# One transformer layer on one core: the last tiles' scaling on ScalarE, and four regroupings in the order of the work

## The reference

```
x = layernorm(x + attention(x))          # 2 x 1024 tokens, D = 512, 16 heads of 32, causal
x = layernorm(x + ffn(x))                # no gain or bias in either layer norm, eps 1e-5
attention: qkv = x @ w_qkv.T + b_qkv; softmax(q k.T / sqrt(32) + causal) v; @ w_out.T + b_out
ffn:  relu((x @ sign(up).T) * up_scale) @ sign(down).T * down_scale * output_scale   # 2048 hidden
```

## Time and profile before

| | |
|---|---|
| median of three runs | 750.09 us |
| the three runs | 747.69, 750.09, 751.0 us |
| the profiled execution | 748.02 us |
| its span, first to last instruction | 746.3 us |
| busy share of the span: PE, DVE, ACT, POOL | 96%, 56%, 43%, 50% |
| mean granted TensorE clock | 0.992 of full speed |

### The profile page before, as it was taken

The page is one execution under the profiler, slowest core; times in us unless marked ns, Lnnn a source line. Parts: engine busy times, 40 slices in busy tenths (PEclk is TensorE's granted clock), DMA queues, the critical chain, the costliest instruction groups (busy, mean ns, idle before and its releaser), DMA issues.

```text
span 746.3 us, 11995 instructions
## 1 busy us (share of the span) xinstructions
PE 714.2 (96%) x4136; PEld 513.9 (69%) x4136; DVE 419.1 (56%) x1024; ACT 323.9 (43%) x647; POOL 374.1 (50%) x515
## 2 busy tenths in 40 slices
PE   6899999999999999999999999999899999999994
PEld 4688766666666656666554677688688787878883
DVE  4176466475765838557388542445783368324514
ACT  5211355665556656556555687522322222222211
POOL 4561458395583946739405449551362245223334
PEclk9999999999999999999999999999999999999997
DMA  7975455625545356463767455313215101000101
GB/s 238 291 232 147 125 156 152 161 88 158 169 144 157 108 144 176 112 161 99 205 184 233 151 191 150 106 47 96 72 32 138 29 1 57 1 1 14 43 1 56
DMA packets 47796, 90.03 MB, mean 121 GB/s; under 512 B 5820, under 2 KB 14780, under 8 KB 47608
## 3 DMA queue, kind: packets, MB, share of 16 engines
q1 hardware_dynamic: 38712, 84.02, 37.9%
q10 hardware_dynamic: 9024, 5.24, 2.4%
HBM read 59.38 MB, written 29.61 MB: 119 GB/s over the span
## 4 chain that ended last, share of the span: by engine, by line
PE 86%; DVE 5%; DMA 3%; issue 3%; ACT 2%; POOL 1%; SPq 0%; ACTq 0%; DVEq 0%; POOLq 0%
PE ps_proj L1115 10%; PE ps_heads L1216 9%; PE ps_proj L1267 8%; PE ps_score L1292 7%; PE ps_unit L1267 7%; PE ps_unit L1151 6%; PE ps_unit L1183 5%; PE ps_unit L1238 5%; PE ps_sum L1210 5%; PE ps_score L1183 4%; PE ps_score L1151 4%; PE ps_sum L1292 2%; PE ps_heads L1292 2%; PE ps_unit L1292 2%; PE ps_score L1135 2%
## 5 line engine op out<-in xcount | busy, mean ns | idle before, releaser
L798 POOL TENSOR_TENSOR hid_low<-hid_raw,hid_high 128x512 fp32r<-128x512 f32 (+1 forms) x80 | 89.8, 1122 | 174.0 <-DVE hid_high L1049 165.9
L855 ACT ACTIVATE probs<-ps_unit 128x512 f32<-128x512 f32 (+3 forms) x214 | 102.2, 490 | 85.1 <-PE ps_unit L1183 80.9
L761 POOL TENSOR_SCALAR_AFFINE_SELECT probs<-probs 128x128 f32<-128x128 f32 x256 | 73.9, 304 | 79.8 <-ACT probs L855 76.0
L855 ACT ACTIVATE probs<-ps_score 128x512 f32<-128x512 f32 (+3 forms) x170 | 82.7, 496 | 64.7 <-PE ps_score L1183 61.8
L961 DVE CUSTOM_DVE_ANT_0 ps_unit<-ps_unit,causal 128x128 f32<-128x128 f32 (+3 forms) x162 | 80.5, 514 | 45.9 <-PE ps_unit L1151 45.2
L1049 DVE CAST hid_high<-hid_raw 128x512 fp32r<-128x512 f32 (+1 forms) x80 | 34.5, 432 | 127.7 <-ACT hid_raw L918 127.2
L1151 PE MATMUL ps_unit<-stack 96*128 96x512 f32 (+3 forms) x242 | 82.9, 354 | 4.4 <-DMA stack<-qk_parts 1.7
L1216 PE MATMUL ps_heads<-probs,v_rows 128*32 128x512 f32 (+3 forms) x768 | 79.8, 492 | 0.0
L1183 PE MATMUL ps_unit<-stack 98*128 98x512 f32 (+2 forms) x214 | 76.8, 362 | 0.6 <-ACT probs L855 0.5
L755 POOL TENSOR_TENSOR parts<-qk_full,parts 128x512 fp32r<-128x512 f32 x32 | 41.2, 1288 | 65.6 <-ACT parts L834 65.6
L774 POOL TENSOR_TENSOR added<-added,probs 128x512 f32<-128x512 f32 x56 | 71.8, 1291 | 0.0
(11 more groups left out here) (216 smaller groups left out, 1462.8 us busy)
## 6 DMA issues: line engine op xcount, KB each, us to landing
stack<-qk_parts SPq DMA_DIRECT2D x96, 256.0 KB, 4.7
qk_parts<-parts SPq DMA_DIRECT2D x32, 512.0 KB, 2.9
v_all<-h_even ACTq DMA_DIRECT2D x16, 256.0 KB, 3.4
v_rows<-v_all SPq DMA_DIRECT2D x8, 512.0 KB, 4.2
heads_t<-heads_sb SPq DMA_DIRECT2D x16, 256.0 KB, 2.6
x_tile<-x_rows SPq DMA_DIRECT2D x16, 256.0 KB, 4.8
raw<-up_w SPq DMA_DIRECT2D x8, 512.0 KB, 3.6
raw<-down_w SPq DMA_DIRECT2D x8, 512.0 KB, 3.9
```

Source lines behind the costliest of these rows:

```text
L761: nc.gpsimd.affine_select(out=tile, in_=tile, compare_op=ALU.is_ge, fill=0.0, base=0, pattern=[[1, P]], channel_multiplier=-1).then_inc(s_ ...
L798: nc.gpsimd.tensor_tensor(parts2[1][:, (HM * s + n) % 3, 0:tokens(s)], full[:, n % 2, 0:tokens(s)], parts2[0][:, (HM * s + n) % 3, 0:token ...
L855: nc.scalar.activation(probs[:, (NP * s + n) % RING, 0:width], bank(what, s, n)[:, off:off + width], ACT.Exp, scale=SCALE).then_inc(s_exp, 1)
```

## The change

Five things are changed.

1. For the last chunk, `out` no longer runs on DVE alone. DVE makes a small offset, `off2 = -mean * rstd` (one column), and ACT writes `z = z * rstd + off2` in place in `z_sb`; the store reads `z_sb`. The last four tiles no longer use `out_sb`. ACT's square root for these tiles is issued with `ln2` instead of with `out`. `mom2`, `std2` and `rstd2` have four columns instead of two, and the wait of the statistics for an older `out` is gone.
2. `ln2` and `out` of the first chunk's tiles 0 and 1 move from slots 12.0 to 13.9 of round 1 to slots 0.2, 0.7, 2.9 and 3.4 of the round behind it, which readers may count as the third (it carries the second chunk). The `scale` pieces of the third chunk start there 0.6 slots later.
3. The first chunk's `attn` of tile 0 starts 1.1 slots sooner, and its `y` 0.9 slots sooner. Its first four matmuls need only the high part of w_out, so the wait for the low part (`s_wol`) moves to the fifth.
4. The first chunk's `turn` pieces stand 0.5 to 0.7 slots later.
5. Round 0's `up` and `down` stand 0.5 and 0.4 slots later, 1.93 instead of 1.95 apart.

```diff
-            put((late + 44.6, late + 47.4, last + 2.4, last + 5)[i] + 0.22 * m, "attn", 0, 12 * i + m)
+            put((late + 43.5, late + 47.4, last + 2.4, last + 5)[i] + 0.22 * m, "attn", 0, 12 * i + m)
...
-        put((last + 13.2, last + 13.7, last + 14.8, last + 15.3)[i], "turn", 0, i)
+        put((last + 13.8, last + 14.4, last + 15.3, last + 15.9)[i], "turn", 0, i)
...
-                put(end + (1.05 if r else 10.8) + q, "ln2", i, q)
-                put(end + (1.95 if r else 11.7) + q, "out", i, q)
+                put(end + 1.05 + q if r else FIRST_UP + 16.2 + 2.7 * q, "ln2", i, q)
+                put(end + 1.95 + q if r else FIRST_UP + 16.7 + 2.7 * q, "out", i, q)
...
                     sp.wait_ge(s_o, TT * s + n + 1)
-                    sp.dma_start(out[s * HALF + n * P:s * HALF + (n + 1) * P, :], out_sb[:, n % 2, :]).then_inc(s_os[n % 2], 16)
+                    src = z_sb[:, n, :] if s == CH - 1 else out_sb[:, n % 2, :]
+                    sp.dma_start(out[s * HALF + n * P:s * HALF + (n + 1) * P, :], src).then_inc(s_os[n % 2], 16)
...
-                if what == "out":
+                if what == ("ln2" if s == CH - 1 else "out"):
                     act.wait_ge(s_mom2, TT * s + n + 1)
-                    nc.scalar.activation(std2[:, n % 2:n % 2 + 1], mom2[:, n % 2, 1:2], ACT.Sqrt, bias=eps[:, :]).then_inc(s_sq2, 1)
+                    nc.scalar.activation(std2[:, n:n + 1], mom2[:, n, 1:2], ACT.Sqrt, bias=eps[:, :]).then_inc(s_sq2, 1)
+                if what == "out" and s == CH - 1:
+
+                    act.wait_ge(s_off, n + 1)
+                    nc.scalar.activation(z_sb[:, n, :], z_sb[:, n, :], ACT.Identity, bias=off2[:, n:n + 1],
+                                         scale=rstd2[:, n:n + 1]).then_inc(s_o, 1)
...
                     dve.wait_ge(s_rs, rs)
+                    if s == CH - 1:
+
+                        nc.vector.tensor_scalar(off2[:, k], mom2[:, n, 0:1], rstd2[:, k], -1.0,
+                                                ALU.mult, ALU.mult).then_inc(s_off, 1)
+                        continue
                     wait(dve, s_os[n % 2], 16 * ((TT * s + n) // 2))
...
-                            pe.wait_ge(s_wol, 2)
...
+                    if s == 0 and n == DC:
+                        pe.wait_ge(s_wol, 2)
```

More of the change, by code:

```diff
@@ L229, in plan @@
         for m in range(12):
-            put((late + 44.6, late + 47.4, last + 2.4, last + 5)[i] + 0.22 * m, "attn", 0, 12 * i + m)
-        put((late + 47.3, last + 2.1, last + 5.1, last + 7.8)[i], "y", 0, i)
+            put((late + 43.5, late + 47.4, last + 2.4, last + 5)[i] + 0.22 * m, "attn", 0, 12 * i + m)
+        put((late + 46.4, last + 2.1, last + 5.1, last + 7.8)[i], "y", 0, i)
         put(last + 9.9 + 0.1 * i, "norm1", 0, i)
-        put((last + 13.2, last + 13.7, last + 14.8, last + 15.3)[i], "turn", 0, i)
+        put((last + 13.8, last + 14.4, last + 15.3, last + 15.9)[i], "turn", 0, i)
     put(last + 9.8, "std1", 0)
@@ L237, in plan @@
         for m in range(HM):
-            put(t + m if r else last + 15.6 + 1.95 * m, "up", r, m)
+            put(t + m if r else last + 16.1 + 1.93 * m, "up", r, m)
             if r < len(ROUNDS) - 1 or m < HM - 2:
-                put(t + m + 2.5 if r else last + 20.5 + 1.95 * m, "down", r, m)
+                put(t + m + 2.5 if r else last + 20.9 + 1.93 * m, "down", r, m)
         if r == len(ROUNDS) - 1:
@@ L243, in plan @@
                 put(t + 17, "finish", i, q)
-        end = t + 17.55 if r else FIRST_UP + 1.2
+        end = t + 17.55 if r else FIRST_UP + 1.6
         for q in tiles:
@@ L261, in plan @@
                 if i:
-                    put(t + (0.1 if i == 1 else -1.4) + 0.5 * q, "scale", i + 1, q)
+                    put(t + (0.7 if i == 1 else -1.4) + 0.5 * q, "scale", i + 1, q)
                 put(t + (2.2 + 0.7 * q if i else 0.3 * q - 0.8), "split", i + 1, q)
@@ L396, in build @@
         rstd1 = sb(top, "rstd1", [P, TT], FP32)
[L397 to L399 removed]
+        mom2 = sb(top, "mom2", [P, TT, 2], FP32)
+        std2 = sb(top, "std2", [P, TT], FP32)
+        rstd2 = sb(top, "rstd2", [P, TT], FP32)
+        off2 = sb(top, "off2", [P, TT], FP32)
         late_inv = sb(top, "late_inv", [P, 48], FP32)
@@ L1071, in _ @@
                     dve.wait_ge(s_bn, bn)
-                    wait(dve, s_o, TT * s + n - 1)
-                    nc.vector.bn_aggr(mom2[:, n % 2, :], stats[:, 1, :]).then_inc(s_mom2, 1)
+                    nc.vector.bn_aggr(mom2[:, n, :], stats[:, 1, :]).then_inc(s_mom2, 1)
                 if what == "out":
-                    k = slice(n % 2, n % 2 + 1)
+                    k = slice(n, n + 1)
                     dve.wait_ge(s_sq2, TT * s + n + 1)
```

6 lines of the change are left out of this document (2 added, 4 removed).

## The result

The changed kernel takes 741.95 us in the median of 6 executions (740.74 to 743.27), before 749.86, also of 6 (the three shown above and three more): ratio 0.9897 with the 95% interval 0.9876 to 0.9917. The two profiled executions differ by 6.4: 748.02 and 741.63, spans 746.3 and 739.9.

A forecast was written before the change was run, and what follows sets the result against it. TensorE, busy 96% of the span, was taken as the bound, losing time only in waits and the tail. Terms -1.0 - 1.7 + 1.8 - 1.6 = -2.5, put on a mean of 749.2, gave 746.7 us; range 744.2 to 750.3.

The forecast's parts named there:

- Edits 3 to 5: Early output matmuls, turns and round 0: attn's wait for y goes (-1.13), some 0.2 given back; -1.0 us together.
- Edit 2, leaving round 1: End of round 1: without the moved DVE work the turn's wait for its norm goes, the next wait stays; -1.7 us.
- Edit 2, arriving: Next round: the moved DVE work makes TensorE wait on z and behind the last low part; +1.8 us.
- the "about 1" behind the last low part: Third chunk's projection in the next round: TensorE waits about 1 us more for DVE's last low part.
- 0.5 of holds that might dissolve: Next round: some GpSimd holds already inside DVE's 12.87 us of busy time may vanish; 0.5 us.
- Edit 1, the tail: Behind the last matmul: ScalarE's scaling shortens the last tiles' chain, with no wait for a store; -1.6 us.
- Rival C: Tail: GpSimd holds DVE's one-column offset, so the tail gives only -1.0; sum -1.9, 747.3 us; chance 0.17.
- Rival A: Next round: moved tiles find gaps and give back only 0.5; sum -4.1, 745.1 us; chance 0.20.
- B: Next round: GpSimd and DVE block each other, costing +5.5; total +1.2, 750.4 us; chance 0.15.
- D: Early attn and turns: the waits only move, so those edits give 0; sum -1.5, 747.7 us; chance 0.10.

The follow-up runs named there:

- e1: The kernel before with only the change's widened small-tile storage, which moves the tiles behind it by 32 bytes; instruction order unchanged: 747.88 us, ratio 0.998.
- e3: The kernel before with only two first-chunk tiles' ln2 and out moved to the next round and scale pieces later: 746.81 us, ratio 0.9969.
- e4: The kernel before with only the first output matmuls sooner and the turns and round 0 later: 748.84 us, ratio 0.9986.
- e12: The changed kernel with round 1's last two down pieces and z of tiles 2 and 3 right behind the fourth turn: 741.97 us, ratio 0.9883.
- e11: The kernel before with round 1's last two down pieces and z of tiles 2 and 3 right behind the fourth turn: 747.24 us, ratio 0.9949.
- e10: The kernel before with down_sb alone moved by 32 bytes: 747.36 us, ratio 0.9972.
- e13: The kernel before with all of TensorE's large tiles placed at 96 modulo 256 bytes: 746.41 us, ratio 0.9948.

## Why the prediction was wrong, point by point

The gain was 5.2 more than the sum had (7.7 by the ratio against 2.5). Two terms stood in it at nothing that were not nothing: the placement (-1.5 by e1) and the clock behind the pair of waits (-1.3 by e3). Of the terms that it priced, edit 2's arrival failed (+1.8 where +0.8 came), and the early edits gave 0.5 more in the trace, while the tail gave 0.2 less. That explains about 4.2; the other 1.0 lies within the interval and has no cause shown.

- **Edits 3 to 5, -1.0.** Half right: -0.8 by 430 us near the forecast, with the small new waits, and -0.7 at 467 that I had not looked for, since I did not follow GpSimd's queue past the low parts. That e4's time also came out at -1.0 is luck: its interval takes in no change as well as the 1.5 of the trace.
- **Edit 2, leaving round 1, -1.7.** Right: -1.8, and the second wait stayed at 1.41.
- **Edit 2, arriving, +1.8.** The priced step that failed most. The 0.8 at `z` came to the tenth; the "about 1" behind the last low part did not. I had named 0.5 of holds that might dissolve and put none of it in the sum. These groups of DVE in after, 526.55 to 542.85 us (count, busy us, mean ns):

```profile
L1012 DVE TENSOR_TENSOR t_even_low<-heads_raw,t_even_high 128x512 fp32r<-128x512 f32 x4 | 5.1, 1282 | 0.1
L1074 DVE TENSOR_TENSOR z_sb<-z_sb,h_even 128x512 f32<-128x512 f32 x3 | 3.1, 1050 | 0.0
L1007 DVE TENSOR_TENSOR heads_raw<-heads_raw,spread_sb 128x512 f32<-128x512 f32 x4 | 2.7, 683 | 0.0
```

  In the stretch of before the same lines had these means:

```profile
L1004 DVE TENSOR_TENSOR t_even_low<-heads_raw,t_even_high 128x512 fp32r<-128x512 f32 x4 | 6.1, 1538 | 0.3
L999 DVE TENSOR_TENSOR heads_raw<-heads_raw,spread_sb 128x512 f32<-128x512 f32 x4 | 3.7, 957 | 0.0
```

  The eight operations that were there already cost 7.8 instead of 9.8: 2.0 us of holds by GpSimd dissolved when the order changed. Against them stands one new hold. Of the two moved norms the first took its plain time and the second was held. Timeline of DVE in after:

```profile
529.12 0.55 DVE L1093 TENSOR_SCALAR out_sb<-z_sb,mom,rstd 128x512 f32<-128x512 f32 x1
...
537.29 1.55 DVE L1093 TENSOR_SCALAR out_sb<-z_sb,mom,rstd 128x512 f32<-128x512 f32 x1
```

  Net the holds fell by 1.0, which is the missing 1.0; the 0.45 between the last low part and `attn` is as long as before. I did not separate what the shorter idle for the square roots (0.4 instead of 0.6) adds. The bound is real all the same: e12 ran into it.
- **Edit 1, the tail, -1.6.** Measured -1.4 in the trace. Rival C fell: the offset at 733.39 took 0.21 within GpSimd's 4.98 us of additions, as long as the three that came after their end. The Trainium skill (VectorE: DVE Perf Modes, with Vector Engine (DVE) Microarchitecture Reference, performance modes) puts its condition for both ports in terms of a dimension of more than one element; I had stretched it to one column. The norm of 512 columns in the earlier trace rows agrees with 1.17, and the one column was not held. My price for ScalarE's scaling was too low: 0.81, not 0.62, since the row I took it from has no scale or bias that is read from a tile. The Trainium skill (ScalarE: Activation LUTs, What ACT_TABLE_LOAD costs) says that each bias or scale read from a one-column tile adds some 93 ns, by which two of them make 0.81 of the row's 0.62; the trace agrees.
- **What was not in the sum.** First the clock. I priced the turn's wait at its length, but it stood right ahead of another, and TensorE's clock fell behind the pair in five of eight profiled executions: some -1.3 more by e3. That breaking the pair raises the clock is shown by 12 executions of e3 and 12 of e11 (0.993 in both against 0.990 and 0.989), and by the profiles; the size is an estimate from e3 (2.3 timed, 1.04 in waits) with an interval from 0 to 2.6. Second the placement, -1.5 by e1, which no wait shows.
- **The sum anew.** Early edits -1.5 (trace), edit 2 -1.0, its clock -1.3, tail -1.4, placement -1.5: -6.7 against the measured 7.7 (6.2 to 9.3). The 1.2 between the traces ahead of 400 us are not a part: at 400 us the traces of e1, e3, e4, e10, e11 and e13, whose order is that of before up to there, lie from 2.2 sooner to 2.3 later than its trace. I put the kernel before at 749.2, 0.4 to 0.7 below the medians that stood beside e1 and the change.
- **Rival A,** -4.1 with 0.5 given back, was nearest to the waits: with the tail they make -3.9 (0.8 given back, 1.5 from the early edits). B, C and D fell: the round gave back 0.8 and not 5.5, the offset was not held, and the early edits were worth 1.5 in the trace.

What stays open: why places modulo 256 bytes matter to the step, why they hardly do so in the attention part, and what the 1.0 between the sum anew and the time is. Whether `stack` lands sooner at multiples of 64 bytes (median 4.4 to 4.5 us against 4.5 to 4.7) or by chance was not separated.

## What to carry to other kernels

An edit that only resizes a small tile moves every tile behind it: where a time changes in code that was not edited, compare the distances of matmuls in both traces first, and run the storage alone. Price a wait together with its neighbours on TensorE, since two waits in a row can cost the clock behind them as well. And where two engines hold each other up, a load measured in one order is no load of the next: 2 of 10 us went away here by order alone, and 1 came back on a moved operation.
